# Batch 0's turned maxima, three transposed scores and unread products in the ramp to attention

## The reference, cut to what matters

```python
def _L0_ffn_ref(...):            # x: 2048 x 128
    shared_out = _swiglu(x, shared_gate, shared_up, shared_down)
    top_id = jnp.argmax(x @ gate_w.T, axis=-1)          # one of 8 experts a token
    score = jax.nn.sigmoid(jnp.max(logits, axis=-1))
    ...                                                  # routed_out: swiglu of x*score by the chosen expert
    return shared_out + routed_out

def _L0_attn_ref(...):           # 16 heads of 8 features
    q, k, v = ...                # projections; q and k rotated (rope)
    scores = jnp.einsum('blhd,bshd->bhls', q, k) / math.sqrt(D_HEAD)
    weights = jax.nn.softmax(scores, axis=-1)
    out = jnp.einsum('bhls,bshd->blhd', weights, v)
    return out @ W_o.T

x = x + 0.5 * _L0_ffn_ref(_layernorm(x), ...)
x = x + _L0_attn_ref(_layernorm(x), ...)
x = x + 0.5 * _L0_ffn_ref(_layernorm(x), ...)
```

## Time and profile before

| what | value |
|---|---|
| median of 3 runs | 324.81 us (321.85 to 330.67) |
| profiled execution | 324.82 us, span 323.0 us |
| mean granted TensorE clock | 0.943 of 2.4 GHz |
| busy: PE, DVE, ACT, POOL | 273.5, 214.4, 178.3, 160.3 us |

### The profile page before, as it was taken

The page is one execution under the profiler, slowest core; times in us unless marked ns, Lnnn a source line. Parts: engine busy times, 40 slices in busy tenths (PEclk is TensorE's granted clock), DMA queues, the critical chain, the costliest instruction groups (busy, mean ns, idle before and its releaser), DMA issues.

```text
span 323.0 us, 6423 instructions
## 1 busy us (share of the span) xinstructions
PE 273.5 (85%) x2046; PEld 152.9 (47%) x2046; DVE 214.4 (66%) x607; ACT 178.3 (55%) x428; POOL 160.3 (50%) x312
## 2 busy tenths in 40 slices
PE   0699979999875979898989898787998998999940
PEld 0575655666531323344344334343644655666630
DVE  6966443447769896898888899798445684344432
ACT  6136214555554486989798979667347441544420
POOL 4426742666745383848484855413003673366660
PEclk9999999999975597999999999899979999999995
DMA  6995136112167006060907061500000115401145
GB/s 179 214 282 203 49 91 140 44 41 67 42 129 172 18 3 131 3 130 2 119 14 132 2 132 35 98 3 2 2 0 18 34 49 130 116 36 43 41 145 164
DMA packets 53264, 26.27 MB, mean 81 GB/s; under 512 B 36752, under 2 KB 50832, under 8 KB 52976
## 3 DMA queue, kind: packets, MB, share of 16 engines
q1 hardware_dynamic: 50736, 20.74, 29.5%
q0 software_dynamic: 2496, 5.13, 4.4%
HBM read 10.29 MB, written 7.71 MB: 56 GB/s over the span
## 4 chain that ended last, share of the span: by engine, by line
PE 49%; POOL 19%; DVE 13%; issue 10%; DMA 4%; ACT 3%; SPq 1%; POOLq 0%; DVEq 0%
PE bank L1119 42%; POOL y_by_token L384 6%; DVE negmax L902 6%; POOL xn L465 3%; POOL rem L435 3%; POOL xs_sorted L375 2%; PE bank L1128 2%; PE bank L1295 2%; PE bank L1253 2%; POOL rstd L460 1%; DMA x<-in_x 1%; POOL parts L442 1%; POOL rot L428 1%; DVE stats L724 1%; DVE rc L917 1%
## 5 line engine op out<-in xcount | busy, mean ns | idle before, releaser
L902 DVE TENSOR_REDUCE negmax<-bank 128x2 f32<-128x512 f32 x128 | 83.1, 682 | 14.2 <-PE bank L1119 13.6
L626 ACT ACTIVATE probs<-bank 128x512 f32<-128x512 f32 x128 | 72.0, 601 | 21.7 <-PE bank L1119 21.7
L1119 PE MATMUL bank<-qkT 64*128 64x256 bf16 x512 | 56.8, 288 | 14.3 <-DVE negmax L902 11.2
L384 POOL DMA_INDIRECT y_by_token<-ys,xg x46 | 44.9, 976 | 42.4 <-issue 25.1
L375 POOL DMA_INDIRECT xs_sorted<-xs,slot x32 | 31.7, 992 | 38.7 <-ACT xs L555 22.3
L1119 PE MATMUL bank<-rgu,xgT 128*128 x92 | 47.2, 596 | 0.7 <-ACT xgT L594 0.7
L869 DVE TENSOR_TENSOR rh<-rsg,bank 128x256 f32<-128x256 f32 x46 | 19.3, 420 | 42.0 <-ACT rsg L602 40.0
L1119 PEld LDWEIGHTS bank<-qkT 64*128 64x128 bf16 x512 | 17.3, 96 | 57.3 <-DVE negmax L902 36.9
L602 ACT ACTIVATE rsg<-bank 128x256 f32<-128x256 f32 x46 | 17.7, 384 | 38.4 <-PE bank L1119 38.4
L1119 PE MATMUL bank<-probs,vx 128*32 128x256 f32 x512 | 36.6, 406 | 0.4 <-ACT probs L626 0.4
L1119 PE MATMUL bank<-xnT,shgu 128*128 128x512 f32 x64 | 31.2, 632 | 0.0
(11 more groups left out here) (126 smaller groups left out, 437.5 us busy)
## 6 DMA issues: line engine op xcount, KB each, us to landing
rgu<-in_rgu SPq DMA_DIRECT2D x1, 2048.0 KB, 19.3
xg<-xs_sorted SPq DMA_DIRECT2D x6, 258.0 KB, 4.5
xs_sorted<-xg SPq DMA_DIRECT2D x1, 1483.5 KB, 15.5
xg<-xs_sorted SPq DMA_DIRECT2D x6, 193.5 KB, 3.3
x<-in_x SPq DMA_DIRECT2D x4, 256.0 KB, 4.8
rdn<-in_rdn SPq DMA_DIRECT2D x1, 1024.0 KB, 15.9
xs<-y_by_token SPq DMA_DIRECT2D x8, 128.0 KB, 2.8
xs<-y_by_token SPq DMA_DIRECT2D x4, 256.0 KB, 4.5
```

What stands on the lines that cost most here:

```text
L384: g.indirect_dma_start(y_dram, bass.IndirectOffsetOnAxis(ap=xg[:, j, D:ROW].bitcast(U32), axis=0), ys[:, j, :], None, bounds_check=N + SLO ...
L626: a.activation(probs[:, h % 8, :], stbank[st_bank(i, h)][:], ACT.Exp, scale=float(DH) ** -0.5).then_inc(exp_done, 1)
L902: v_.tensor_reduce(negmax[:, w, :, h0 + k], sbank[(h0 + k) % 2][:].rearrange("p (t s) -> p t s", t=2), AX.X, ALU.max, negate=True).then_in ...
L1119: return t_.matmul(o_, l, r, start=start, stop=stop, **k)
```

## The change

Six edits, all in the ramp.

- ScalarE, turn -1: `copy_queries("ma")` stands at step 10 instead of 12, in turn -1 alone.
- TensorE, first routed stage: at j = 22 and at j = 23 three unread products each into `gT_bank[0]`, once a wait for the last copy of turned rows is past.
- TensorE, turn -2: four unread products into `pvbank`, ahead of `turn_normalised`.
- TensorE, turn -1: one unread product ahead of the unit at each of steps 3 to 15; at step 13 three more, then `turn_parts("ma")` (so ahead of unit 10, not behind it), then four more.
- TensorE, turn -1, step 13: behind these, still ahead of unit 10, the transposed scores of heads 0 to 2 of batch 0, with their wait for ScalarE's copy.
- TensorE, turn 0: steps 0 to 2 don't issue transposed scores any more. `scores_t` and `score_t_part` take the batch as an argument for this.

```diff
@@ scalar, attention_turn
-                    if n == 12 and T.m:
+                    if n == (10 if i == -1 else 12) and T.m:
                         copy_queries("ma")
@@ tensor, routed
                 def turn(j, u, has):
+                    if n == 0 and j == SLOT_TILES - 1:
+                        pe.wait_ge(gT_copied, SLOT_TILES)
+                    if n == 0 and j >= SLOT_TILES - 1:
+                        for _ in range(3):
+                            mm(gT_bank[0][:, 0:TABB_COLS], onesb, tabb[:])
@@ tensor, attention_turn
+                def turn_parts_ahead():
+
+                    pe.wait_ge(m_split, 2 * (i + 1) + 1)
+                    turn_parts("ma")
+
+                def unread_ahead(k):
+
+                    for _ in range(k):
+                        mm(pvbank[:, 0:TABB_COLS], onesb, tabb[:])
...
-                def scores_t(h):
+                def scores_t(b, h):
 
                     if h % HH == 0:
-                        pe.wait_ge(emptied[("ma", "mb")[h // HH]], i + 1)
-                    if H * i + h >= 3:
-                        pe.wait_ge(exp_done, H * i + h - 2)
+                        pe.wait_ge(emptied[("ma", "mb")[h // HH]], b + 1)
+                    if H * b + h >= 3:
+                        pe.wait_ge(exp_done, H * b + h - 2)
...
                 if i == -2:
+                    unread_ahead(4)
                     turn_normalised()
                     return
...
                 for n in range(H):
                     unit = T.unit(n)
+                    if i == -1 and n >= 3:
+                        unread_ahead(1)
+                    if i == -1 and n == 13:
+                        unread_ahead(3)
+                        turn_parts_ahead()
+                        unread_ahead(4)
+                        for h in range(3):
+                            scores_t(0, h)
+                            score_t_part(0, h, 0)
+                            score_t_part(0, h, 1)
+                    own = T.e and (i or n >= 3)
                     if unit:
                         scores(*unit)
                         score_part(*unit, 0)
-                    if T.e:
-                        scores_t(n)
-                        score_t_part(n, 0)
+                    if own:
+                        scores_t(i, n)
+                        score_t_part(i, n, 0)
                     if unit:
                         score_part(*unit, 1)
-                    if T.e:
-                        score_t_part(n, 1)
+                    if own:
+                        score_t_part(i, n, 1)
...
-                    if n == 13 and T.m:
-                        pe.wait_ge(m_split, 2 * (i + 1) + 1)
-                        turn_parts("ma")
+                    if n == 13 and T.e and T.m:
+                        turn_parts_ahead()
```

More of the change, by code:

```diff
@@ L1324, in score_part, with score_t_part @@
                         ins.then_inc(s_filled, 1)
-                def scores_t(h):
+                def scores_t(b, h):
                     if h % HH == 0:
-                        pe.wait_ge(emptied[("ma", "mb")[h // HH]], i + 1)
-                    if H * i + h >= 3:
-                        pe.wait_ge(exp_done, H * i + h - 2)
-                def score_t_part(h, k):
+                        pe.wait_ge(emptied[("ma", "mb")[h // HH]], b + 1)
+                    if H * b + h >= 3:
+                        pe.wait_ge(exp_done, H * b + h - 2)
+                def score_t_part(b, h, k):
+                    u = b % 2
                     rows, half, r = slice(h % 2 * KROWS, (h % 2 + 1) * KROWS), h // HH, h % HH // 2
-                    ins = mm(stbank[st_bank(i, h)][:, k * L:(k + 1) * L], qkT[u][rows, half, 1, r, k * P:(k + 1) * P], qkT[u][rows, half, 0, r, :])
+                    ins = mm(stbank[st_bank(b, h)][:, k * L:(k + 1) * L], qkT[u][rows, half, 1, r, k * P:(k + 1) * P], qkT[u][rows, half, 0, r, :])
                     if k:
```

## The result

The changed kernel's four executions have a median of 329.98 us (327.57 to 331.66), beside 325.78 (321.85 to 330.67) for four of the kernel before: ratio 1.0216, 95% interval 1.0159 to 1.0272. The forecast was 322.5, range 318.8 to 326.4. The profiled execution took 330.42 us, its span is 328.6, 5.6 more than before.

The account below looks back on a forecast made before the run. The prediction took the chain of waits through the ramp from routed experts to attention, with TensorE largely at half clock, as the bound. Its terms, 0.05 + 0.5 - 1.4 - 0.35 - 0.3 - 0.77, gave -2.3: 322.5 us, range 318.8 to 326.4.

Parts of the forecast that it names:

- (a): Routed stage, three unread products each at j = 22 and j = 23: cost +0.05 us, bounds 0 to 0.25.
- (b): Turn -2, four unread products ahead of turning the normalised rows: cost +0.5 us, bounds 0.35 to 1.08.
- (c): Ramp, from turning the normalised rows to the first maximum, if the clock holds: 5.82 us becomes 4.4, -1.4.
- (d): Ramp, eight maxima at a full-clock cadence of 0.60 us: 4.8 us and small gaps instead of 5.19, -0.35.
- (e): From maximum 7's end to unit 13's maximum, with an added wait for ScalarE's copy: -0.3 us, bounds -0.6 and -0.15.
- (f): Turn 0, unit 13's maximum to the end of rope(1), at full clock: 5.63 us becomes 4.86, -0.77.
- rival 3: Loss of clock only moves, a 3.4 us half-clock stretch falling into turn 0: about 324 us, chance 0.20.
- Rival 1: Clock holds through the ramp and also at 122.25 us, for another 1.9 us: 320.6 us, chance 0.18.
- Rival 2: Unread products in the ramp don't hold the clock and are paid for at 1.2 GHz: 328.0 us, chance 0.12.

Follow-up runs that it names:

- r5: Changed kernel plus one unread product at step 1 and four at step 2 of turns 6 and 7: 320.66 us, 0.9899 of the kernel before.
- r7: Changed kernel loaded once more without any edit: 324.09 us, 0.9934 of the kernel before.
- r1: Changed kernel loaded once more without any edit: 339.46 us, 0.9885 of the kernel before.
- r16: Changed kernel loaded once more without any edit, beside the delayed forms: 338.67 us, 1.0120 of the kernel before.
- r2: Kernel before, loaded once more without any edit: 333.13 us, 0.9874 of itself.
- r8: Kernel before, loaded once more without any edit: 323.94 us, 0.9988 of itself.
- r15: Kernel before plus four copies of unused rows on VectorE at step 11 of turn 6: 338.28 us, 1.0119 of the kernel before.
- r9: Repeat of r5, the changed kernel with unread products at steps 1 and 2 of turns 6 and 7: 332.16 us, 0.9923 of the kernel before.

## Why the prediction was wrong

The ramp went by the forecast's steps. What failed is the sentence behind the chain, that bringing the second rope's end forward "moves POOL's chain, and so the rest, as long as nothing else is late": the sum stopped at turn 0 and took everything behind it as a block that shifts. Turn 7 isn't such a block. From its queries to the last routed tile it is about 86 us or about 92, by when the clock falls.

The changed kernel's chain of waits and TensorE's timeline, beside the earlier trace rows:

```profile
97.17 4.79 DVE negmax L902 x8
101.96 0.03 issue
101.99 0.21 DVE parts L1026
...
105.50 1.60 POOL xn L465 x2
...
108.26 4.71 PE bank L1119 x13
...
114.02 0.41 DVE rs L919 x2
...
121.66 0.31 POOL parts L417
```

```profile
88.84 0.65 PE L1119 MATMUL bank<-tabb 128*128 128x384 bf16 x3
89.53 0.44 PE L1258 MATMUL bank<-tab,rh 128*128 128x128 f32 x2
...
92.39 0.81 PE L1119 MATMUL bank<-tabb 128*128 128x384 bf16 x4 [0.48 <-DVE ys L872]
93.03 0.38 PE L1420 MATMUL bank<-tab,xn 128*128 128x128 f32 x2
...
104.77 0.83 PE L1119 MATMUL bank<-qkT 64*128 64x256 bf16 x8 [0.45 <-ACT qkT L632]
```

- (a) Right: the transposes behind the three products come 1.14 us behind the expert products before them, 1.13 before. 0.0 for 0.05.
- (b) Right: from the last expert products (91.21) to the turn (93.03) 1.82 us, 1.40 before. +0.42 for +0.5; four in a row take 0.64, start to start with the turn, so 0.16 each, as the Trainium skill had it (TensorE: Matmul & The Clock Gate, Back-to-back issue gap) and not the 0.27 of the earlier trace rows, which is the distance to a score product.
- (c) 93.03 to 97.17 is 4.14 us: -1.68 for -1.4.
- (d) 97.17 to 101.99 is 4.82: -0.37 for -0.35.
- (e) 101.99 to unit 13's maximum at 108.70 is 6.71: -0.57 for -0.3, the forecast's better end. TensorE waits 0.45 for ScalarE's copy and VectorE then 0.19 for unit 10, not 0.57. But the way to the turned rows didn't get shorter. The forecast had POOL's rows "no longer late"; in the profile TensorE still waits 0.46 for them (107.24), and from the split to their turn it is 5.25 us, 5.26 before. Nearly all of the 0.57 lies behind that turn, where VectorE has now taken unit 12's maximum already.
- (f) 108.70 to 114.42 is 5.72: +0.09 for -0.77, since the clock fell at 107.2; this much was rival 3. In r5's profile, with no fall from 92 to 112, it is 4.6.

The turn of POOL's rows, in the kernel before and in the changed one:

```profile
106.30 0.66 PE L1404 MATMUL bank<-tab,xn 128*128 128x128 f32 x2 [0.23 <-POOL xn L465]
```

```profile
107.24 0.41 PE L1420 MATMUL bank<-tab,xn 128*128 128x128 f32 x2 [0.46 <-POOL xn L465]
```

Sum of these in the profile -2.1, forecast -2.3. That the sums agree so well is in part luck, since (c) and (e) came out 0.3 us better each than forecast and (f) 0.9 worse. Its worth didn't reach the total. The ramp's 2 us vanish beside falls of the clock elsewhere: 1.2 us at the end of turn 0, 1.6 in the routed stage, 6.0 for those of turn 7.

Two rivals came true in part. Rival 1's sign, a full clock at 120 to 126, is there and brought 1.2 us of its 1.9. Rival 3 had the direction of what happened, "the loss of clock only moves", and priced it at one stretch of 3.4 us in turn 0. Rival 2 read the earlier trace rows rightly, that 235 to 238.5 was at half clock among unread products with TensorE busy, but put it to the ramp and not to turn 7 itself. The row was in hand; its stage wasn't asked what a fall costs it.

On the verdict itself: four loads of the changed kernel gave medians of 1.013, 1.004, 0.999 and 1.010 of the kernel before's beside them, two loads of the kernel before 0.985 and 0.999. So the change brings no gain and costs 0 to 1%, less than two loads of one kernel differ by. The 2.2% come from a load in which all four executions (327.57 to 331.66) were at the height of r7's upper group, while two of the kernel before's four were left out of the ratio.

Open stays whether the changed kernel loses turn 7 more often, and why. All four profiles of it without a hold have the 10.2 and 6.8 us (first one, r1, r7, r16), none of the three of the kernel before has more than 3.4 (first, r2, r8); both are the same code there. But seven profiles are few. On the chip of r7, executions of 327.8 us or more are 5 of 12 of the changed kernel, and 7 of 35 of the kernel before (r8 and beside it). That a delay brought the long loss into the kernel before (r15) shows only that it can occur there too. Which part of the change would set it, no run shows.

## What to carry to other kernels

Before an early gain is added up, look at every later stage in which TensorE is busy throughout and the profile shows a fall of the clock, and ask what a longer one there costs; that price can be several times the gain. Five or ten unread products in the holes ahead of such a stage did more than the thirty in the ramp: all seven loads with a hold, whatever the ramp, had medians at 0.989 to 0.992 of the kernel before, and the six without a hold or a delay that carry the whole change or none of it 0.985 to 1.013. The changed kernel with the hold (320.66 us beside 324.29) and the kernel before with the hold (321.52) are equally good within what can be told. Repeat loads, not only executions: two loads of one kernel differed by 1.3%.

## What the runs showed of the hardware

The same program takes 324 to 326 us on some chips and 335 to 338 on others (medians of the kernel before). The stretches at half clock lasted from 3.4 us to 17.0 (r15). The time that TensorE was busy says little of whether the clock falls or comes back: it fell behind 9.60 us with 9.60 busy (r9, 226.5 to 236.1), and stayed at half over 10.30 us with 10.30 busy (first profile of the changed kernel, turn 7).
